# A state-space block with a gated feed-forward: cube and du of batch 0 on VectorE, two quarters of C fetched before the diagonals

## The reference

```
x   = x + tanh(g_xattn) * ssm(ctx, layernorm(x))
x   = x + tanh(g_ffn)   * ffn(layernorm(x))
ssm: v = silu(conv4(in_proj(ctx)) + conv_b)            # [b, 256 channels, 256 tokens]
     dt_low, B, C = split(x_proj(v), 8, 16, 16)
     dt = softplus(dt_proj(dt_low) + dt_b)
     state[n] = state[n] * exp(dt * A[n]) + dt * v * B[n]      # along the tokens, n = 0..15
     y = sum_n state[n] * C[n] + D * v ;  y = y * silu(z)
ffn: inner = rmsnorm(relu(x1)^2 * x3) ; both operands of both products are rounded to a grid of 127 steps
```

## Time and profile before

| | us |
|---|---|
| median of 3 runs | 190.58 (190.2 to 190.88) |
| the profiled execution's own time | 192.25 |
| its span | 190.4 |
| TensorE busy | 174.0 (91%) |
| VectorE busy | 160.5 (84%) |
| ScalarE busy | 152.7 (80%) |
| GpSimd busy | 124.0 (65%) |
| mean granted clock of TensorE | 0.973 of full |

### The profile page before, as it was taken

The page is one execution under the profiler, slowest core; times in us unless marked ns, Lnnn a source line. Parts: engine busy times, 40 slices in busy tenths (PEclk is TensorE's granted clock), DMA queues, the critical chain, the costliest instruction groups (busy, mean ns, idle before and its releaser), DMA issues.

```text
span 190.4 us, 3401 instructions
## 1 busy us (share of the span) xinstructions
PE 174.0 (91%) x1098; PEld 139.4 (73%) x1098; DVE 160.5 (84%) x263; ACT 152.7 (80%) x388; POOL 124.0 (65%) x88
## 2 busy tenths in 40 slices
...
PEclk9999965899999999999999999999999999999999
...
GB/s 125 329 390 278 2 160 300 398 37 28 136 384 235 288 41 2 9 191 261 104 0 0 103 130 51 281 40 296 0 106 280 3 0 0 0 5 57 0 57 57
DMA packets 32530, 24.59 MB, mean 129 GB/s; under 512 B 19344, under 2 KB 25216, under 8 KB 32512
## 3 DMA queue, kind: packets, MB, share of 16 engines
...
HBM read 21.08 MB, written 3.28 MB: 128 GB/s over the span
## 4 chain that ended last, share of the span: by engine, by line
PE 62%; POOL 12%; DVE 8%; issue 8%; ACT 6%; DMA 1%; POOLq 0%
PE m_ps L1057 22%; PE w_ps L1111 10%; PE y_ps L1081 10%; PE w_ps L1128 7%; POOL hb L409 6%; PE w_ps L1119 3%; PE w_ps L1034 2%; ACT dA L689 2%; PE y_ps L1069 2%; DVE xc L815 2%; PE y_ps L987 2%; POOL gw L424 2%; PE w_ps L1026 1%; DVE xstat L856 1%; POOL u L392 1%
## 5 line engine op out<-in xcount | busy, mean ns | idle before, releaser
L409 POOL TENSOR_TENSOR hb<-hb,cs 128x1024 f32<-128x1024 f32 x31 | 73.9, 2406 | 8.4 <-DVE hb L891 5.1
L891 DVE TENSOR_TENSOR_SCAN hb<-dA,m_ps 128x1024 f32<-128x1024 f32 x30 | 67.6, 2273 | 6.5 <-PE m_ps L1057 6.4
L1057 PE MATMUL m_ps<-bd,duT 128*128 128x256 f32 (+1 forms) x216 | 58.6, 416 | 1.7 <-ACT duT L704 1.2
L689 ACT ACTIVATE dA<-dt,nega 128x255 f32<-128x255 f32 (+1 forms) x144 | 54.8, 461 | 0.0
L1057 PEld LDWEIGHTS m_ps<-bd,duT 128*128 128x128 f32 x216 | 40.4, 196 | 11.9 <-issue 4.8
L1081 PE MATMUL y_ps<-identf,hb 128*128 128x128 f32 x256 | 31.5, 273 | 0.0
L1081 PEld LDWEIGHTS y_ps<-identf,hb 128*128 128x128 f32 x256 | 29.0, 141 | 2.2 <-issue 1.6
L1111 PE MATMUL w_ps<-w13T,xqT 128*128 128x352 bf16 x192 | 30.4, 313 | 0.0
L1111 PEld LDWEIGHTS w_ps<-w13T,xqT 128*128 128x128 bf16 x192 | 18.5, 98 | 9.7 <-issue 0.4
L1128 PE MATMUL w_ps<-w2T,iqT 128*128 128x256 bf16 x144 | 16.5, 273 | 0.0
L424 POOL TENSOR_TENSOR gw<-gg,normw 128x704 f32<-128x704 f32 x7 | 12.6, 1795 | 5.0 <-DVE gg L933 5.0
...
## 6 DMA issues: line engine op xcount, KB each, us to landing
cs<-c_rows SPq DMA_DIRECT2D x16, 512.0 KB, 6.2
bd<-b_diag SPq DMA_DIRECT2D x14, 512.0 KB, 6.5
...
```

The lines of the kernel that those rows point to most:

```text
L409: E.tensor_tensor(h_g, h_g, cs[:, s0:s0 + sn, l0:l0 + ln], ALU.mult).then_inc(hc_end if (b, i, h) == OUT_END else hc_ok[h], 1)
L689: last = act_fn(dA_g[:, s, 1:ln], dt[:, p, h, l0 + 1:l0 + ln], ACT.Exp, scale=nega[:, h, s0 + s:s0 + s + 1])
L891: V.tensor_tensor_scan(hb[:, k % 3, h], dA[:, k % 2, h].rearrange("p n l -> p (n l)"), m_ps[:, h], 0.0, ALU.mult, ALU.add).then_inc(scan_o ...
L1057: last = T.matmul(m_q[:, :, c * P - l0:(c + 1) * P - l0], duT[:, p, c, h * P:(h + 1) * P], bd[:, (s0 + sn // 2 * q) // GN, c, n0:n0 + sn / ...
```

## The change

The changed kernel computes the same with the same code for every step; the tables differ. `cubic/0.0`, `cubic/0.1`, `du/0.0` and `du/0.1` go from the string of GpSimd to that of VectorE. `cget/0.0` and `cget/0.1` go ahead of the four `bget` of batch 0. `WARM` has 68 transposes in place of 66, and they stand elsewhere. The strings of all engines have a new order; the diff shows the lines on the first part of the program (that of SyncE whole as it is now).

```diff
-WARM = (8, 10, 8, 8, 8, 8, 8, 8)
+WARM = (8, 10, 8, 8, 8, 6, 10, 10)
...
     "pe": """
-        ctxT/0.0 winT/0.0 inproj/0.0 ctxT/1.0 inproj/0.1 warm/0.0 warm/0.1 xpwT/0.0 dtwT/0.0 warm/0.2 warm/0.3
-        xdbl/0.0 inproj/1.0 dtproj/0.0 warm/0.4 dtproj/0.1 ctxT/2.0 w/0.0 w/0.1 warm/0.5 w/0.2 duT/0.0 duT/0.1
-        mix0/0.0 w/0.3 xdbl/1.0 mix1/0.0 mix0/0.1 inproj/2.0 mix1/0.1 dtproj/1.0 warm/0.6 warm/0.7 w/0.4 skip/0.0
-        sum0/0.0 mix0/0.2 sum1/0.0 mix1/0.2 w/0.5 sum0/0.1 mix0/0.3 w/0.6 sum1/0.1 mix1/0.3 duT/1.0 sum0/0.2 w/0.7
-        mix0/1.0 mix1/1.0 szT/0.0 sum1/0.2 sum0/0.3 sum1/0.3 mix0/1.1 ctxT/3.0 mix1/1.1 skip/1.0 w/0.8 xdbl/2.0
...
+        ctxT/0.0 winT/0.0 inproj/0.0 inproj/0.1 warm/0.0 ctxT/1.0 xpwT/0.0 warm/0.1 dtwT/0.0 warm/0.2 warm/0.3
+        xdbl/0.0 inproj/1.0 dtproj/0.0 warm/0.4 dtproj/0.1 ctxT/2.0 warm/0.5 w/0.0 w/0.1 duT/0.0 warm/0.6 duT/0.1
+        w/0.2 mix0/0.0 mix1/0.0 w/0.3 xdbl/1.0 mix0/0.1 inproj/2.0 mix1/0.1 dtproj/1.0 mix0/0.2 w/0.4 warm/0.7
+        mix1/0.2 skip/0.0 w/0.5 sum0/0.0 szT/0.0 sum1/0.0 sum0/0.1 sum1/0.1 duT/1.0 mix0/0.3 sum0/0.2 mix1/0.3
+        sum1/0.2 mix0/1.0 w/0.6 mix1/1.0 ctxT/3.0 sum0/0.3 sum1/0.3 mix0/1.1 w/0.7 mix1/1.1 xdbl/2.0 inproj/3.0
...
     "dve": """
-        winT/0.0 conv/0.0 conv/0.1 xstat/0.0 clamp/0.0 xstat/1.0 clamp/0.1 u/0.0 xstat/2.0 u/0.1 xstat/3.0 lowc/0.0
-        dtwT/0.0 gates/0.0 conv/1.0 series/0.0 clamp/1.0 dt/0.0 series/0.1 w_res/0.0 dt/0.1 w_res/0.1 w_res/0.2
-        scan0/0.0 lowc/1.0 w_res/0.3 scan1/0.0 scan0/0.1 scan1/0.1 conv/2.0 series/1.0 cubic/1.0 dt/1.0 scan0/0.2
-        du/1.0 w_res/0.4 scan1/0.2 w_res/0.5 clamp/2.0 scan0/0.3 scan1/0.3 w_res/0.6 scan0/1.0 scan1/1.0 yz/0.0
-        w_res/0.7 x1/0.0 scan0/1.1 scan1/1.1 lowc/2.0 w_res/0.8 scan0/1.2 conv/3.0 absx1/0.0 quant1/0.0 series/2.0
...
+        winT/0.0 conv/0.0 conv/0.1 clamp/0.0 xstat/0.0 clamp/0.1 xstat/1.0 xstat/2.0 u/0.0 u/0.1 xstat/3.0 dtwT/0.0
+        lowc/0.0 gates/0.0 conv/1.0 series/0.0 cubic/0.0 dt/0.0 series/0.1 cubic/0.1 du/0.0 dt/0.1 clamp/1.0
+        w_res/0.0 du/0.1 w_res/0.1 scan0/0.0 scan1/0.0 w_res/0.2 lowc/1.0 w_res/0.3 scan0/0.1 scan1/0.1 conv/2.0
+        w_res/0.4 series/1.0 cubic/1.0 dt/1.0 scan0/0.2 du/1.0 scan1/0.2 clamp/2.0 scan0/0.3 w_res/0.5 scan1/0.3
+        scan0/1.0 scan1/1.0 yz/0.0 x1/0.0 w_res/0.6 scan0/1.1 lowc/2.0 w_res/0.7 scan1/1.1 scan0/1.2 absx1/0.0
...
     "pool": """
-        cubic/0.0 dtadd/0.0 cubic/0.1 du/0.0 dtadd/0.1 du/0.1 u/1.0 w_lo/0.0 diag/0.0 w_lo/0.1 out0/0.0 w_lo/0.2
-        out1/0.0 out0/0.1 out1/0.1 dtadd/1.0 sz/0.0 w_lo/0.3 out0/0.2 out1/0.2 w_lo/0.4 out0/0.3 out1/0.3 out0/1.0
...
+        dtadd/0.0 dtadd/0.1 u/1.0 w_lo/0.0 diag/0.0 w_lo/0.1 out0/0.0 out1/0.0 sz/0.0 out0/0.1 out1/0.1 dtadd/1.0
+        w_lo/0.2 out0/0.2 out1/0.2 w_lo/0.3 out0/0.3 out1/0.3 w_lo/0.4 out0/1.0 u/2.0 sz/1.0 out1/1.0 w_lo/0.5
...
     "sp": """
-        l_ctx/0.0 l_x/0.0 l_xpw/0.0 l_g/0.0 l_dtw/0.0 zero/0.0 l_dtb/0.0 l_alog/0.0 l_w13/0.0 l_d/0.0 cput/0.0
-        bput/0.0 bget/0.0 bget/0.1 cget/0.0 bget/0.2 cget/0.1 l_w2/0.0 l_nw/0.0 bget/0.3 bput/1.0 cput/1.0 cget/0.2
-        bget/1.0 cget/0.3 bget/1.1 cget/1.0 bget/1.2 bget/1.3 cget/1.1 cget/1.2 cget/1.3 bput/2.0 cput/2.0 bget/2.0
-        cget/2.0 bget/2.1 bget/2.2 bget/2.3 mput/3.0 cget/2.1 cput/3.0 cget/2.2 bput/3.0 cget/2.3 bget/3.0 bget/3.1
...
+        l_x/0.0 l_dtw/0.0 l_ctx/0.0 l_xpw/0.0 l_g/0.0 zero/0.0 l_dtb/0.0 l_w13/0.0 l_alog/0.0 l_d/0.0 cput/0.0 bput/0.0 cget/0.0 cget/0.1 bget/0.0 bget/0.1 bget/0.2 bget/0.3 bput/1.0 bget/1.0 bget/1.1 cput/1.0 cget/0.2 cget/0.3 cget/1.0 l_w2/0.0 bget/1.2 cget/1.1 cget/1.2 cget/1.3 bget/1.3 bput/2.0 bget/2.0 bget/2.1 bget/2.2 cput/2.0 cget/2.0 l_nw/0.0 bget/2.3 cput/3.0 cget/2.1 cget/2.2 bput/3.0 bget/3.0 mput/3.0 cget/2.3 bget/3.1 cget/3.0 cget/3.1 bget/3.2 mget/3.1 cget/3.2 store/0.0 store/0.1 bget/3.3 cget/3.3 store/1.0 store/1.1 store/2.0 store/2.1 store/3.0 store/3.1
```

More of the change, by code:

```diff
@@ L93 @@
-        mix0/1.2 inproj/3.0 dtproj/2.0 mix1/1.2 mix0/1.3 sum0/1.0 sum1/1.0 sum0/1.1 xqT/0.0 sum1/1.1 up/0.0 up/0.1
-        mix1/1.3 duT/2.0 szT/1.0 up/0.2 sum0/1.2 mix0/2.0 up/0.3 sum1/1.2 sum0/1.3 sum1/1.3 mix1/2.0 szT/2.0
-        xdbl/3.0 mix0/2.1 skip/2.0 mix1/2.1 sum0/2.0 dtproj/3.0 mix0/2.2 xqT/1.0 sum1/2.0 up/1.0 iqT/0.0 sum0/2.1
-        mix1/2.2 up/1.1 up/1.2 mix0/2.3 up/1.3 mix1/2.3 sum1/2.1 duT/3.0 iqT/0.1 mix0/3.0 sum0/2.2 mix1/3.0 sum1/2.2
-        sum0/2.3 sum1/2.3 szT/3.0 down/0.0 down/0.1 iqT/1.0 skip/3.0 mix0/3.2 sum0/3.0 mix1/3.2 xqT/2.0 sum1/3.0
```

68 lines of the change are left out of this document (36 added, 32 removed).

## The result

| | before | changed |
|---|---|---|
| median, us | 190.73 (190.2 to 191.49) | 199.94 (198.69 to 202.12) |
| ratio | | 1.0428 [1.0359, 1.0497] |
| the profiled execution's own time, us | 192.25 | 198.84 |
| its span, us | 190.4 | 197.0 |
| VectorE busy, us | 160.5 (84%) | 162.7 (83%) |

The changed kernel is slower by 4.3% by the ratio (8.2 us) and by 9.2 us by the medians: about four times the 2.1 us that I had forecast, and outside the range. The spans differ by 6.6 us. The rest of the 9.2 is where the two profiled executions stand: that of before lies 1.5 us over its median, that of the changed kernel 1.1 under. What follows explains the 6.6 of the traces.

What follows compares the result with a forecast made beforehand. TensorE and VectorE have no slack, and the first diagonals gate the first scan. 0.33 + 1.4 - 0.81 + 0.56 + 1.0 - 0.4 = +2.1 us, put on the median: 192.7 us, range 189.0 to 194.5.

Steps and rivals of the forecast that it cites:

- du behind the diagonals, value 0: Opening: du about 2 us sooner on VectorE, hidden because the first mix waits for the diagonals; value 0.
- C ahead of the diagonals, +1.4: Opening: two quarters of C queued ahead of the first diagonals make them land later, +1.4 us (0 to 2.8).
- low late, +0.33: Opening: dtwT copied before low delays the writes of C and B and the first diagonals, +0.33 us (0 to 0.4).
- The clock: Opening: TensorE's granted clock falls as before, low from before mix0/0.0 to about 35 us.
- the rival in which the clock holds: Opening: clock stays at 2.4 GHz up to mix0/0.0, which takes 1.89 for 3.75 us; 189.4 us, chance 0.20.
- The gap before the second scan, -0.81: VectorE's 0.81 us idle before its second scan closes, with mix1/0.0 right behind mix0/0.0; -0.81 us.
- w_res/0.2, +0.56: w_res/0.2, formerly done in VectorE's idle opening, now stands in the dense part; +0.56 us.
- The third quarter of C, +1.0: Batch 0: C's third quarter is issued later, lands at 55.7, GpSimd waits 1.5 us; +1.0 us (0 to 2.5).
- The rest of the new order, -0.4: VectorE's middle: half of the 0.82 us gap before yz/1.0 may be swallowed; -0.4 us (-0.8 to 0).
- The rival in which C costs its far end, 194.2: C's third quarter lands 7.2 us after its own issue, at 56.4, with late diagonals; +3.6, 194.2 us, chance 0.20.

Runs made afterwards that it cites:

- E: Kernel before with only cube and du of batch 0 moved from GpSimd to VectorE: 191.43 us, ratio 1.0026.
- K: Changed kernel, loads as before, first two C fetches behind diagonals, later two ahead of batch 1's, scale2/1.0 ahead of yz/2.0: 198.68 us, ratio 1.0413.
- Q: K with outscale/1.0 on VectorE moved later, to just ahead of final/1.0: 197.03 us, ratio 1.0259.
- C: Changed kernel with third and fourth quarter of C of batch 0 fetched ahead of batch 1's diagonals: 197.41 us, ratio 1.0351.
- G: Changed order on the compute engines, SyncE's order of before, and scale2/1.0 ahead of yz/2.0 on VectorE: 192.53 us, ratio 1.0055.

## Why the prediction was wrong

The sum was +2.1 us; the traces differ by +6.6. The side was right, the size wrong by a factor of three on the traces and of four on the ratio. Term by term:

- **du behind the diagonals, value 0: right.** The gate was the diagonals, and E, with nothing else moved, has the first scan at 32.96.
- **C ahead of the diagonals, +1.4, and low late, +0.33: right in sum, by luck.** First scan forecast at 34.7, measured 34.62. The parts were others: the write of B was issued 0.94 later (forecast 0.33; low was copied at 15.46 for 14.73), it took 0.48 longer until the diagonals could be issued (forecast nothing), from there to the mix it was 0.64 more (forecast 1.4), and mix0/0.0 took 0.36 less (forecast nothing). I had let C only queue ahead of the diagonals and taken the landing of B as given. The Trainium skill's page "DMA: Bandwidth & Descriptors" ("Queues, rings and completion order") had drawn me towards 2.8 for the queue; the traces show 1.0 in the mean. And in the new order without C ahead the scan stands at 31.8 (mean of nine), 1.1 before the old one, which I had not seen: 0.4 are quicker diagonals, 0.7 a clock that is higher during mix0/0.0.
- **The clock: right.** I had it low from before mix0/0.0 to about 35. In windows of the changed kernel (columns as in rows 2) it is still full while TensorE stands idle, and falls before the first mix starts at 31.09:

```profile
29.00:30.00 1.00, 0.00 (x0) 0.00 (x0) 0.00 (x0) 1.00 (x4) 1.00 (x2) 1.00 1.01 346
30.00:31.00 1.00, 0.00 (x0) 0.00 (x0) 0.00 (x0) 1.00 (x4) 1.00 (x2) 0.79 0.96 340
31.00:32.00 1.00, 0.91 (x2) 0.84 (x3) 0.00 (x0) 0.64 (x2) 0.24 (x1) 0.50 1.06 410
34.00:35.00 1.00, 1.00 (x6) 0.87 (x6) 0.38 (x1) 0.00 (x0) 0.00 (x0) 1.00 0.04 12
```

  It is back by 34, so that the 16 passes took 5.12 us: 7.5 at the lower level by the earlier trace rows, 3.8 at the full. mix0/0.0 took 3.39 of them, for 3.75 before; the rival in which the clock holds did not come. It did in K, where the diagonals came at 28 and TensorE's gap was 1.29 us. Timelines of TensorE of K, then of Q:

```profile
28.07 3.69 PE L1058 MATMUL m_ps<-bd,duT 128*128 128x256 f32 x16 [1.29 <-DMA bd<-b_diag]
```

```profile
28.81 5.20 PE L1058 MATMUL m_ps<-bd,duT 128*128 128x256 f32 x16 [2.35 <-DMA bd<-b_diag]
```

  Two things about the clock I had wrong on the way. It wasn't full from the start before: the transposes up to 11.5 us took 0.22 each, though the earlier trace rows has a 9 there. And in the changed kernel it was also low from 20 to 24 us (0.50 in 21 to 23), and rose again while TensorE did nothing but transposes. The trace speaks here, too, against the Trainium skill's page "TensorE: Matmul & The Clock Gate" ("Part 4: PE-mode transpose"), by which transposes don't count as busy time in the same way.
- **The gap before the second scan, -0.81, and w_res/0.2, +0.56: too timid.** The second scan gained 2.0 us on the first (36.82 for 37.18 before, with the first at +1.68), but 1.1 of it are low's copy and w_res/0.3, which now come behind it. At scan0/0.3, where the changed kernel is 0.1 us ahead of before (56.25 for 56.36), 1.8 of the first scan's delay are made up; the sum had 0.25.
- **The third quarter of C, +1.0: the mechanism right, the size wrong.** It was issued at 48.20 and GpSimd waited for it until 56.70, where I had 55.7: a landing after 8.4 us, behind two fetches of diagonals and a write of rows. I had bounded it at 7.2. From scan0/0.3 to scan1/0.3 the kernel lost 3.6 us; C takes 3 of them back.
- **The rest of the new order, -0.4: the step that failed.** I looked in VectorE's middle for gaps to close, found one, and let batch 3 stand at nothing. It lost 3.1. I read the order of names there as equal work. What I missed is that VectorE and GpSimd hold each other, so that the same names in another phase take another time. 1.9 of the 3.1 is the one hold of gt (2.22 for 0.30), and 0.9 is absmax/1.1, whose place moved from before the cut to behind it. No experiment gives the 1.9 back: in G, with gt at 0.79, quant2/1.0 is held in its place and the last stage is 0.9 us shorter.

Put together: +1.7 at the first scan, -1.8 up to scan0/0.3, +3.6 at the third quarter of C, -0.3 up to scan1/1.0, +0.3 in batches 1 and 2, +3.1 in batch 3: +6.6.

The rival in which C costs its far end, 194.2, was nearest in its mechanism. It fell short for the same reasons.

The holds could have been seen before. In the trace of before there are eight VectorE products that take 0.3 to 2 us over their least time while a GpSimd product runs, 5.5 us in all. The Trainium skill's page "SBUF — State Buffer" ("Who interferes with whom") states the rule: a VectorE instruction with two inputs in SBUF, or in a two-port mode, and a GpSimd instruction that reads SBUF get in each other's way, and whoever issues first has the shared ports for its whole instruction. The traces agree: 2.22 against 0.30 for gt, and in the kernel before GpSimd's product at 138.98, started 0.1 us after VectorE's ru, took 2.68 for 2.36. Steps with an operand in PSUM, as yz, x1, the gates and the scans, take no more than 0.25 us over their least time in any trace that is used here.
